# Another order of the staged keys in DRAM, other read patterns, and a seventh product in two chained attention blocks

## The reference, cut to what matters

```python
# block 1, per batch
nx = layer_norm(x) ; q, k, v = nx @ Wq, ctx @ Wk, ctx @ Wv
evidence = softmax(q @ k.T * H ** -0.5) @ v
combined = concat(nx, evidence, cond)
h = silu(combined @ e_w1 + e_b1) ; routed = sum(softmax(combined @ router_W) * (h @ e_w2 + e_b2))
x1 = x + sigmoid(silu(combined @ gate_w1) @ gate_w2) * (routed @ out_w + out_b)
# block 2, per batch: 16 heads, dh = 8
q = ada_ln(x1) @ Wq + bq ; k, v = split(ada_ln(ctx) @ Wkv + bkv)
out = softmax(q @ k.T / sqrt(dh)) @ v          # per head
y = x1 + out @ Wp + bp
```

## Time and profile before

| | us |
|---|---|
| median of 3 runs | 241.36 |
| lowest and highest | 240.87 and 243.3 |
| the profiled execution | 241.37 |
| its span | 239.5 |
| TensorE busy | 186.6 |
| VectorE busy | 141.5 |
| ScalarE busy | 120.3 |
| GpSimd busy | 51.3 |

### The profile page before, as it was taken

One profiled execution on the slowest core, in us unless ns is written; L12 is line 12 of the kernel. 1 busy time (PEld: TensorE's weight loads), 2 busy tenths in 40 slices (PEclk: granted clock), 3 DMA queues, 4 the chain that ended last, 5 costly groups with the idle time before them and its releaser, 6 DMA issues.

```text
span 239.5 us, 4440 instructions
## 1 busy us (share of the span) xinstructions
PE 186.6 (78%) x1534; PEld 116.3 (49%) x1538; DVE 141.5 (59%) x386; ACT 120.3 (50%) x263; POOL 51.3 (21%) x81
## 2 busy tenths in 40 slices
...
PEclk9999999999855699996899997599999659999999
...
GB/s 128 344 247 6 5 0 0 18 66 72 118 60 36 89 92 19 37 53 62 20 4 33 4 66 77 54 8 3 28 41 92 55 18 3 45 5 23 4 3 22
DMA packets 10871, 12.32 MB, mean 51 GB/s; under 512 B 1480, under 2 KB 9570, under 8 KB 10466
## 3 DMA queue, kind: packets, MB, share of 16 engines
...
...
q10 hardware_dynamic: 58, 0.01, 0.0%
...
## 4 chain that ended last, share of the span: by engine, by line
PE 55%; DMA 14%; DVE 7%; ACT 6%; issue 6%; SPq 6%; POOL 4%; ACTq 0%; DVEq 0%; POOLq 0%
PE ps L712 50%; DMA k_st<-k_scr 10%; PE ps L715 5%; DMA q_st<-mT 4%; SPq L398 3%; ACT probs L663 3%; DVE mparts L1260 3%; SPq L408 2%; POOL cn L505 1%; DVE xn L1244 1%; DVE bias_rows L1022 1%; POOL qr L537 1%; ACT L569 1%; POOL qp L535 1%; POOL kr L522 0%
## 5 line engine op out<-in xcount | busy, mean ns | idle before, releaser
L1260 DVE TENSOR_REDUCE mparts<-ps 128x1 f32<-128x512 f32 x128 | 81.7, 682 | 41.4 <-PE ps L712 41.2
L663 ACT ACTIVATE probs<-ps 128x512 f32<-128x512 f32 x128 | 66.6, 603 | 26.5 <-PE ps L712 26.2
L712 PE MATMUL ps<-k_st,q_st 48*128 48x512 bf16 x128 | 24.3, 415 | 27.6 <-issue 13.5
L712 PE MATMUL ps<-probs,vtile 128*32 128x256 f32 x512 | 34.9, 395 | 0.8 <-ACT probs L663 0.7
L712 PE MATMUL ps<-q_st,k_st 51*128 51x256 bf16 x256 | 23.1, 285 | 10.3 <-DMA q_st<-mT 9.2
L712 PEld LDWEIGHTS ps<-k_st,q_st 48*128 48x128 bf16 x128 | 6.2, 95 | 44.6 <-issue 19.8
L712 PEld LDWEIGHTS ps<-probs,vtile 128*32 128x32 f32 x512 | 14.2, 112 | 13.9 <-ACT probs L663 4.0
L712 PEld LDWEIGHTS ps<-q_st,k_st 51*128 51x128 bf16 x256 | 9.8, 97 | 22.7 <-DMA q_st<-mT 10.3
L630 ACT ACTIVATE tz<-ps 128x512 f32<-128x512 f32 (+1 forms) x16 | 8.7, 544 | 21.7 <-PE ps L712 21.7
L1194 DVE SCALAR_TENSOR_TENSOR hT<-tz,ps 128x512 f32<-128x512 f32 (+1 forms) x16 | 9.9, 617 | 10.0 <-ACT tz L630 9.8
L712 PE MATMUL ps<-nxT,w 128*128 128x256 f32 x48 | 14.3, 380 | 0.0
(11 more groups left out here) (166 smaller groups left out, 301.1 us busy)
## 6 DMA issues: line engine op xcount, KB each, us to landing
...
q_scr<-qp SPq DMA_DIRECT2D x12, 64.0 KB
...
```

The costliest lines, as they stand in the source:

```text
L663: A.activation(probs[:, g % 2, j, half * 2 * T:(half + 1) * 2 * T], bank("unit", b, n, side=two), ACT.Exp).then_inc(s["e"], 1)
L712: return nc.tensor.matmul(out, lhsT, rhs, start=start, stop=stop)
L1260: V.tensor_reduce(cells(mparts, g, 0)[:, t, two, u:u + 1], bank("tile", b, n, side=two), AX_X, ALU.max, negate=True).then_inc(s["mx"], 1)
```

## The change

`k_scr` gets the order of the partitions with the parts side by side: [slot][head of the slot][dimension][part][512] instead of [part][head][dimension][slot][512]. k_out writes each part into it, 128 rows of 1 KB. k_in reads for i = 0 and i = 1 all three parts, as 24 rows (dimension, part) of eight 1 KB pieces each (one per slot), and for i = 2 only the first part, 8 rows. q_in has the dimension as its outermost loop and the repetition inside. For i = 1 there are now three products instead of two: seven in all, 56 partitions (59 with the maxima). In the partitions of a product group the dimension now varies slower than the part. The seventh product is q part 1 with k part 2.

```diff
-ROW_OF = (0, 3 * DH, 5 * DH)
-KR = 6 * DH
+ROW_OF = (0, 3 * DH, 6 * DH, 7 * DH)
+KR = ROW_OF[NP]
...
-        k_scr = nc.dram_tensor("k_scr", (2, NP, 2, DH, NS, S), BF16, kind="Internal").ap()
+        k_scr = nc.dram_tensor("k_scr", (2, NS, 2, DH, NP, S), BF16, kind="Internal").ap()
...
-            return slice(SIDE * two + ROW_OF[i], SIDE * two + ROW_OF[i] + (NP - i) * DH)
+            return slice(SIDE * two + ROW_OF[i], SIDE * two + ROW_OF[i + 1])
...
-                sp.dma_start(k_scr[b % 2, j].rearrange("two d s t -> s (two d) t"), kp[:, j, :]).then_inc(s_kscr, 16)
+                sp.dma_start(k_scr[b % 2, :, :, :, j].rearrange("s two d t -> (s two d) t"), kp[:, j, :]).then_inc(s_kscr, 16)
...
-                             k_scr[b % 2, 0:NP - i, two].rearrange("j d s t -> j d (s t)")).then_inc(s_kst[b % 2], 16)
+                             k_scr[b % 2, :, two, :, 0:NP if i < NP - 1 else 1]
+                             .rearrange("s d j t -> (d j) s t")).then_inc(s_kst[b % 2], 16)
...
+                one = q_scr[b % 2, i, two].rearrange("d s t -> d (s t)")
                 sp.dma_start(q_st[places(two, i), b % 2, :, :],
-                             q_scr[b % 2, i, two].rearrange("d s t -> d (s t)").unsqueeze(0)
-                             .to_broadcast([NP - i, DH, NS * T])).then_inc(s_qst[b % 2], 16)
+                             one.unsqueeze(1).to_broadcast([DH, NP, NS * T]) if i < NP - 1 else one).then_inc(s_qst[b % 2], 16)
```

All five lists of ORDER are written anew. The tasks are the same; their order and the banks differ. SyncE's new list:

```diff
+        brows k_out.0.0 k_out.0.1 k_out.0.2 q_out.0.0 q_out.0.1 k_in.0.0 q_out.0.2 k_in.0.1 k_in.0.2 k_in.0.3 k_in.0.4
+        q_in.0.0 q_in.0.1 q_in.0.2 k_in.0.5 q_in.0.3 q_in.0.4 q_in.0.5 k_out.1.0 k_out.1.1 k_out.1.2 k_in.1.0 k_in.1.1
+        k_in.1.2 k_in.1.3 k_in.1.4 k_in.1.5 k_out.2.0 k_out.2.1 k_out.2.2 q_out.1.0 q_out.1.1 q_out.1.2 q_in.1.0
+        q_in.1.1 q_in.1.2 q_in.1.3 q_in.1.4 q_in.1.5 mrow.0.0.0 mrow.0.0.1 mrow.0.1.0 mrow.0.1.1 mrow.0.2.0 mrow.0.2.1
+        mrow.0.3.0 mrow.0.3.1 q_out.2.0 q_out.2.1 q_out.2.2 mrow.1.0.0 mrow.1.0.1 k_in.2.0 k_in.2.1 q_in.2.0 q_in.2.1
+        k_in.2.2 k_in.2.3 q_in.2.2 q_in.2.3 k_in.2.4 k_in.2.5 q_in.2.4 q_in.2.5 mrow.1.1.0 mrow.1.1.1 k_out.3.0
+        mrow.1.2.0 mrow.1.2.1 k_out.3.1 k_out.3.2 mrow.1.3.0 mrow.1.3.1 mrow.2.0.0 mrow.2.0.1 q_out.3.0 q_out.3.1
+        mrow.2.1.0 q_out.3.2 mrow.2.1.1 k_in.3.0 k_in.3.1 q_in.3.0 k_in.3.2 k_in.3.3 k_in.3.4 k_in.3.5 q_in.3.1
+        q_in.3.2 q_in.3.3 q_in.3.4 q_in.3.5 mrow.2.2.0 mrow.2.2.1 mrow.2.3.0 mrow.2.3.1 mrow.3.0.0 mrow.3.0.1
+        mrow.3.1.0 mrow.3.1.1 mrow.3.2.0 mrow.3.2.1 mrow.3.3.0 mrow.3.3.1 store.0 store.1 store.2 store.3""",
```

Of TensorE's new list, the parts with tile.0.0, tile.2.0 and tile.3.0:

```diff
+        eo.1.1@2 s0.2.1@3 kproj.1@7 p0T.2.0@0 tile.0.0@6+5 qm.3@4 hkvT.2@1 tile.0.1@2+3 tile.0.2@0+6 tile.0.3@7+5
...
+        unit.0.15@6+0 tile.1.11@5+2 eo.3.1@7 tile.1.12@4+3 tile.1.13@5+6 tile.1.14@2+0 pv.0.4@1 unit.1.0@4+3 pv.0.5
+        tile.1.15@5+4 rows.1.1@6 unit.1.1@3+2 hkvT.3@1 unit.1.2@6+0 unit.1.3@3+5 pv.0.6@2 tile.2.0@4+1 tile.2.1@6+7
+        kproj.3@0 tile.2.2@3+4 tile.2.3@5+1 pv.0.7 tile.2.4@0+6 rows.1.2@7 unit.1.4@3+2 unit.1.5@7+4 unit.1.6@3+5
...
+        unit.1.15@6+0 vproj.3@2 tile.2.12@4+7 tile.2.13@1+5 pv.1.6@6 tile.2.14@0+4 unit.2.0@3+7 pv.1.7 unit.2.1@1+3
+        tile.2.15@5+7 rows.2.2@0 oT.0.0@2 unit.2.2@4+1 unit.2.3@0+5 oT.0.1@3 unit.2.4@7+4 pv.2.0@1 rows.2.3@2
+        unit.2.5@3+0 tile.3.0@5+7 pv.2.1 tile.3.1@2+4 tile.3.2@5+3 unit.2.6@0+7 oT.1.0@6 tile.3.3@1+2 unit.2.7@0+4
```

More of the change, by code:

```diff
@@ L53 @@
     "pe": """
[L54 to L83, removed]
-    "act": """
[L85 to L101, removed]
@@ new lines @@
+        s0.3.0@4 tile.0.4@2+1 s0.3.1@3 kproj.2@0 p0T.2.1@6 vproj.1@7 tile.0.5@0+5 pc.2@6 xqT.1@2 tile.0.6@7+1
+        tile.0.7@0+5 hid.2.0@6 qproj.1@2 tile.0.8@7+4 tile.0.9@1+0 hid.2.1@5 tile.0.10@2+6 tile.0.11@7+4 hid.2.2@1
+        hid.2.3@0 tile.0.12@2+6 lgT.2@7 eo.2.0@4 rows.0.0@5 eo.2.1@1 tile.0.13@0+2 tile.0.14@6+7 tile.0.15@5+3
+        rows.0.1@4 p0T.3.0@0 p0T.3.1@4 rows.0.2@2 tile.1.0@6+0 tile.1.1@4+7 pc.3@2 tile.1.2@5+3 tile.1.3@6+0 hid.3.0@2
+        unit.0.0@4+7 tile.1.4@5+1 hid.3.1@3 unit.0.1@4+7 tile.1.5@6+0 hid.3.2@5 tile.1.6@4+1 unit.0.2@7+6 xqT.2@0
@@ new lines @@
+        kproj.3@0 tile.2.2@3+4 tile.2.3@5+1 pv.0.7 tile.2.4@0+6 rows.1.2@7 unit.1.4@3+2 unit.1.5@7+4 unit.1.6@3+5
+        rows.1.3@2 pv.1.0@1 pv.1.1 tile.2.5@7+0 tile.2.6@4+3 unit.1.7@6+5 tile.2.7@2+1 pv.1.2@7 unit.1.8@6+0 xqT.3@5
+        rows.2.0@4 pv.1.3 qproj.3@6 tile.2.8@3+5 unit.1.9@2+0 unit.1.10@4+7 tile.2.9@1+6 rows.2.1@3 vproj.2@2
+        unit.1.11@5+0 unit.1.12@4+1 unit.1.13@7+6 pv.1.4@3 tile.2.10@5+0 pv.1.5 tile.2.11@4+1 unit.1.14@7+5
+        unit.1.15@6+0 vproj.3@2 tile.2.12@4+7 tile.2.13@1+5 pv.1.6@6 tile.2.14@0+4 unit.2.0@3+7 pv.1.7 unit.2.1@1+3
@@ L125 @@
     "pool": """
[L126 to L129 removed]
+        vt0 ident identb rsx.0 rsc.0 cn.0 gw2h rsx.1 rsc.1 cn.1 rsx.2 rsx.3 rsc.2 cn.2 rsc.3 cn.3 rs1.0 kp.0.0 kp.0.1
```

92 lines of the change are left out of this document (56 added, 36 removed).

## The result

The changed kernel takes 210.54 us (median of 4 runs, 209.69 to 211.91), against 241.37 us for the kernel before, run beside it on the same chip: a ratio of 0.8715 [0.8648, 0.8782]. The forecast was 207 us with a range of 197 to 220. So the sign and most of the size came as expected, and the time is 3.5 us (1.7%) above the forecast. The profiled execution took 211.91 us, with a span of 210.0 us against the 205.4 of the sum.

A forecast was written before the change was run, and what follows sets the result against it. The prediction took TensorE's stalls on key and query reads carried by few DMA engines as the bound. Its sum, 239.5 - 35.75 + (1.5 + 0 + 1 + 1) - 6.9 + 3 + 2 = 205.4 us of span, gave 207 us, range 197 to 220.

The forecast's parts named there:

- The bound: TensorE's four stretches without matrix work, 35.75 us, two thirds of its idle time, put down to reads on few engines.
- The read time: A batch's twelve reads: 7.7 us of SyncE issue plus 1.9 us for the last to land, 9.6 us instead of 21.
- my upper end: A batch's reads at 122 GB/s, the fastest earlier stretch with copies and reads of this kind: 11.3 us for 1,344 KB.
- The estimate of 7.0 us for the busiest engine: New reads on 12 and 8 engines: the busiest carries 80 KB in 1 KB pieces and 56 KB in 4 KB rows.
- The leftovers: TensorE stalls remaining before the first scores of batches 0 to 3: 1.5, 0, 1 and 1 us.
- unit.1.4: Its wait for a row of maxima, the third stall, would be covered by ten tiles, 13.6 us of VectorE reductions.
- the bare sums of 6.7 and 7.1: TensorE work covering the reads of batches 2 and 3, in us, leaving at most 2.9 and 2.5 before other fill.
- The clock: TensorE's half clock after three stalls would go, returning 6.9 us; the clock fell about 3 us into each idle stretch.
- The charges: Added TensorE waits: 3 us for VectorE's backlog once the stalls are gone, 2 us for tighter packing of the engines.
- Of the rivals, the first: Reads at 122 GB/s take 13.2 us, or TensorE waits for VectorE: 218 us, range 212 to 222; chance 0.20.
- The second: Rival: the reads still go to few engines, with three the load stays about 408 KB; 234 to 246 us, chance 0.03.
- the third: Rival: the key reads' pieces are too small and it gets slower, mostly 243 to 260 us; chance 0.03.

The follow-up runs named there:

- layout_old_order: The changed kernel's layout, reads and seven products, but with the five instruction lists of the kernel before; 215.88 us, ratio 0.9022.
- the kernel with alternating reads: The changed kernel with neighbouring key and query reads going to the two heads of a slot in turn; 208.64 us, 0.8719; once more 206.26 us, 0.8476.
- slots_in_halves: The changed kernel with each key and query read cut in two by slots, earlier waits for the first half and SyncE's list moved; 197.48 us, 0.83.

## Why the prediction was right, and where it was off

*The bound.* Right. The stalls on too few engines were two thirds of TensorE's idle time, and the change took 26 of their 35.75 us away; the changed loops under the old orders took 24 (11.65 are left in *layout_old_order*). The old reads under the new orders kept 35.05.

*The read time: the step that failed.* I put 9.6 us between the first read and the last landing, because "SyncE's own pace" was to be the bound and the last read to land 1.9 us after it. Measured from the first read to tile.b.0: 12.2, 12.7 and 11.7 us. The issue was even cheaper than taken, but the transfer was the bound, near my upper end: 122 GB/s for 1,344 KB, which with the 1.9 us makes 13.2. The mistake was to choose between the bounds by the row of another resource. The row of the same kind of traffic was there, and it measured the right rate; I had used it as the extreme case. The rule for the number of engines, from the Trainium skill ("DMA: Bandwidth & Descriptors", section on why a DMA increments its semaphore by 16), agrees with the direction: 8 or 24 outermost sped the reads up. The estimate of 7.0 us for the busiest engine took for granted that 12 engines run as fast each as a few do; this the trace refutes, 14 GB/s against the 17 and 25 in it.

*The leftovers.* Forecast 1.5 + 0 + 1 + 1 = 3.5 us, measured 2.69 + 0 + 4.21 + 2.84 = 9.7. Batch 1 and unit.1.4 were right. At batches 2 and 3 TensorE's cover was 8.5 and 8.9 us (123.16 to 131.65, 156.35 to 165.26), which is the bare sums of 6.7 and 7.1 and nearly the fill of 1.9 and 1.5 that the step left for waits and other work. So the whole miss at these two is the read time, 12.7 - 9.6 = 3.1 and 11.7 - 9.6 = 2.1 us. In batch 0 TensorE was ready at 64.8 instead of 61.2, late by the head's delay (next section), but this delay hid nothing: it moved the reads as much. The two profiles of the kernel with alternating reads show it, one with the delay and one without: first read at 55.12 and 51.45 us, TensorE ready at 64.63 and 60.95, stalls of 1.46 and 1.73. What made up for most of the longer read is the key chain under the new orders. Without the delay its first read goes out some 3 us before the 54.31 of the kernel before (51.23 in *slots_in_halves*), where the step had only "a little earlier".

*The clock.* Partly right: the 6.9 us came back, but 3.90 and 2.90 us at 0.56 and 0.50 stand behind the first two leftovers. Half of that is lost where TensorE is the bound: 3.90 x 0.44 + 2.90 x 0.50 = 3.2 us. Behind the third, 2.84 us long, it stayed up, though behind the first, 2.69 us long, it fell. So the 3 us at which I had put the fall, from the longer stalls of before, didn't hold: by the windows the clock fell some 2.6 us into the first leftover, some 4.0 us into the second, and not at all in the third.

*The charges.* 5 us for VectorE's backlog and the tighter packing were too much. In the 60.35 us between the first two stalls TensorE is idle for 2.1, about the share of before. *slots_in_halves* shows what the sum is without leftovers: its profiled span is 192.3 us, where mine would be 239.5 - 35.75 - 6.9 = 196.9, without any charge. Of this difference of 4.6 us, 1.6 are in TensorE's busy time (178.1 against 186.6 - 6.9) and 3.0 in its small idle times (14.2 against 52.9 - 35.75).

*What no step had*: a late head (next section), 4 us, of which the half clock there is 3.1.

From there the time after comes together: 192.3 + 9.7 (leftovers) + 3.2 (clock behind them) + 4.0 (head) = 209.2 us against a span of 210.0. Against the sum of 205.4 the leftovers are 6.2 too small, the clock behind them 3.2 and the head 4.0; the charges are 5.0 and the base of 196.9 is 4.6 too large. That leaves 3.8 us, so the total of 207 is near partly by offsets. These are profiled executions; by medians the two kernels are 13.1 us apart rather than 17.7, likely because the clock at the head differs from one execution to the next. The mechanism of the forecast is shown by the runs; its size had their help.

*Other marks that I had named.* TensorE's busy time was to be 175 to 180 us: it is 185.3, mostly the half clock again (178.1 in *slots_in_halves*, at full clock). tile.0.0 was to start near 63: 67.47, of which 4 is the head. No idle stretch over 3 us: one of 4.21. No window with a share near 0.12: nearly right, as only the last 2 us of the first stall show 0.15. VectorE and ScalarE unchanged: 143.2 and 121.0 us, right. Of the rivals, the first had the right mechanism for the reads (transfer at 122 GB/s, 13.2 us) but at 218 the wrong price, since it added its delay to a sum that already had the charges. The second fell (three engines at the 25 GB/s of before would be 75 GB/s, and the reads moved 168), and the third with it: a piece of 1 KB costs nothing that can be measured against one of 8 KB.
